# First attention: reciprocals stored element by element, output product moved, GpSimd gates removed

## The reference, cut to what matters

```python
q, k, v = einsum('bsx,xAnh->Abnsh', input, w)          # b=8, s=512, x=128, 16 heads of 64
q = q + q_bias
a = einsum('bnqh,bnkh->bnqk', q, k) * 64 ** -0.5
a = a + relative_causal(einsum('bnqh,nvh->bnqv', q, emb) * 64 ** -0.5)
a = softmax(where(lower_triangle, a, -1e9), axis=-1)
o = einsum('bnqk,bnkh->bqnh', a, v).reshape(b, s, 1024)
out = o @ (out_kernel * scale) + out_bias
x = layernorm(x + out)
```

## Time and profile before

| | |
|---|---|
| median of 3 runs | 1633.0 us (1631.59 to 1633.61) |
| the profiled execution | 1630.46 us, span 1628.7 us |
| first product of the first attention, last one | 74.78, 763.42 us |
| PE busy | 1351.0 us, 83% |
| VectorE busy | 1305.7 us, 80% |
| ScalarE busy | 947.3 us, 58% |
| GpSimd busy | 921.4 us, 57% |
| mean granted TensorE clock | 0.953 |

### The profile page before, as it was taken

The page is one execution under the profiler, slowest core; times in us unless marked ns, Lnnn a source line. Parts: engine busy times, 40 slices in busy tenths (PEclk is TensorE's granted clock), DMA queues, the critical chain, the costliest instruction groups (busy, mean ns, idle before and its releaser), DMA issues. The chain is left out here.

```text
span 1628.7 us, 36836 instructions
## 1 busy us (share of the span) xinstructions
PE 1351.0 (83%) x11495; PEld 775.6 (48%) x11495; DVE 1305.7 (80%) x2722; ACT 947.3 (58%) x1857; POOL 921.4 (57%) x1203
## 2 busy tenths in 40 slices
PE   4888888888988988886698987489899899997936
PEld 3466656655665656654366665123332333332316
DVE  3799899998999898996788888387777877777834
ACT  2676767776767767773244444157666666665631
POOL 2788988888898989896455555211221231231635
PEclk9899999999999999997699999599999999999978
DMA  5667766565666656564000000411011111101001
GB/s 153 136 152 144 146 145 145 129 154 134 147 145 144 144 139 148 131 147 100 1 1 1 0 0 0 150 48 37 29 35 34 35 32 30 40 27 32 25 8 33
DMA packets 401554, 133.51 MB, mean 82 GB/s; under 512 B 362156, under 2 KB 389793, under 8 KB 401377
## 3 DMA queue, kind: packets, MB, share of 16 engines
q1 hardware_dynamic: 398144, 128.41, 33.2%
q10 hardware_dynamic: 1824, 3.15, 0.6%
q0 software_dynamic: 1536, 1.34, 0.3%
HBM read 37.14 MB, written 13.15 MB: 31 GB/s over the span
## 5 line engine op out<-in xcount | busy, mean ns | idle before, releaser
L565 ACT ACTIVATE prob<-score_ps,nmax 128x512 f32<-128x512 f32 (+3 forms) x512 | 264.8, 525 | 202.7 <-DVE nmax L606 201.9
L1577 DVE TENSOR_REDUCE a_nm<-a_s 128x1 f16<-128x512 f32 x512 | 324.5, 687 | 52.8 <-PE a_s L1349 51.9
L1503 ACT ACTIVATE a_pt<-a_st 128x1024 f32<-128x1024 f32 x256 | 260.7, 1021 | 121.8 <-PE a_st L1367 118.7
L618 DVE SCALAR_TENSOR_TENSOR p<-prob,p 128x1280 f16<-128x1280 f32 x128 | 214.4, 1675 | 44.8 <-ACT p L574 44.8
L1349 PE MATMUL a_s<-a_kop,a_qop 128*128 128x512 f16 x512 | 198.1, 388 | 58.8 <-DVE a_nm L1577 42.3
L606 DVE TENSOR_REDUCE nmax<-score_ps 128x1 f32<-128x512 f32 (+3 forms) x512 | 217.9, 480 | 18.1 <-PE score_ps L486 15.9
L708 POOL TENSOR_TENSOR k_l<-k,k_h 64x512 f16<-64x512 f32 x130 | 191.5, 1473 | 10.9
L483 PE MATMUL score_ps<-k_h,q_h 128*128 128x512 f16 (+3 forms) x512 | 156.5, 306 | 48.5 <-ACT prob L565 28.9
L130 POOL TENSOR_TENSOR gate<-mhalf 128x1 f32<-128x1 f32 (+1 forms) x284 | 85.8, 302 | 190.5 <-ACT k L586 64.4
L708 POOL TENSOR_TENSOR q_l<-q,q_h 128x512 f16<-128x512 f32 x130 | 183.0, 1408 | 10.8
L574 ACT ACTIVATE p<-prob 128x1280 f16<-128x1280 f32 x128 | 162.6, 1271 | 8.5
(11 more groups left out here) (328 smaller groups left out, 3319.2 us busy)
## 6 DMA issues: line engine op xcount, KB each, us to landing
r_bc<-r_parts SPq DMA_DIRECT2D x128, 128.0 KB, 2.8
a_qop<-q_parts SPq DMA_DIRECT2D x32, 128.0 KB
a_kop<-k_parts SPq DMA_DIRECT2D x128, 24.0 KB
x_tok<-in_L_attn_input_dram SPq DMA_DIRECT2D x4, 512.0 KB, 12.4
pt<-p SPq DMA_TRANSPOSE x128, 4.1
r_parts<-rsum SPq DMA_DIRECT2D x128, 2.0 KB, 2.2
e_w<-in_L_ffn_w_dram SPq DMA_DIRECT2D x1, 2048.0 KB, 8.4
q_parts<-a_q_h SPq DMA_DIRECT2D x16, 128.0 KB
```

Of the source, the lines that this page charges most:

```text
L565: ins = nc.scalar.activation(prob[h][:, P_OFF[c]:P_OFF[c] + w], score_ps[u][:, col:col + w], ACT.Exp, bias=nmax[h][:, c:c + 1], accum_out= ...
L618: nc.vector.scalar_tensor_tensor(p16[h][k][:, 1, :], prob[h][:, :], P_SCALE, p16[h][k][:, 0, :], ALU.mult, ALU.subtract).then_inc(p_lo[h], 1)
L1503: nc.scalar.activation(pt[kc % 2][r][:, :, :], st_ps[r][:, :, :], ACT.Exp, scale=1.0 / SC).then_inc(exp_done[r], 1)
L1577: nc.vector.tensor_reduce(nm[g % 2][:, c, hh:hh + 1], s_ps[c % 2][:, :], AX.X, ALU.max, negate=True).then_inc(max_done[c % 2], 1)
```

## The change

Three edits. The store of the reciprocals writes DRAM in the order c, p, which makes it 512 elements of 4 bytes instead of 128 runs of 16; in return `normalise` reads `r_bc` contiguously. `normalise(n - 2)` stands ahead of `low(0, n)` on VectorE. On GpSimd the gate is gone; a semaphore increment stands in its place, and the counts that the subtractions wait for are doubled.

```diff
             def store_r(h, n, k):
...
-                sp.dma_start(r_dram[k, h].rearrange("(q c) -> q c", c=QC), rsum[h][k][:, :]).then_inc(r_stored, 16)
+                sp.dma_start(r_dram[k, h].rearrange("(c q) -> q c", q=P), rsum[h][k][:, :],
+                             allow_slow_non_contiguous=True).then_inc(r_stored, 16)
...
             def normalise(n, k):
...
-                nc.vector.tensor_tensor(o32[:, :].rearrange("p (c q) -> p c q", q=P), pv_ps[:, :].rearrange("p (c q) -> p c q", q=P),
-                                        r_bc[k][:, :].rearrange("p (q c) -> p c q", c=QC), ALU.mult).then_inc(o_done, 1)
+                nc.vector.tensor_tensor(o32[:, :], pv_ps[:, :], r_bc[k][:, :], ALU.mult).then_inc(o_done, 1)
...
                 reciprocals(0, n, k)
-                low(0, n, k)
                 if later(n, 2):
                     normalise(n - 2, k)
+                low(0, n, k)
                 maxima(1, n)
...
-            def split(rows, src, hi, lo, chain_n):
-                pool_gate(nc, m, rows)
+            def split(src, hi, lo, chain_n):
+                pool.sem_inc(pool_steps, 1)
                 nc.gpsimd.affine_select(out=hi, in_=src, compare_op=ALU.is_ge, fill=0.0, base=0,
                                         pattern=[[1, S]], channel_multiplier=0).then_inc(pool_steps, 1)
                 pool.wait_ge(pool_steps, chain_n)
...
-                split(slice(0, P), q32[h][:, :], q_h[h][:, :], q_l[h][:, :], 4 * n + 2 + 2 * h).then_inc(q_split[h], 1)
+                split(q32[h][:, :], q_h[h][:, :], q_l[h][:, :], 8 * n + 4 + 4 * h).then_inc(q_split[h], 1)
...
-                split(r, k32[r, :], m.k_h[h][r, :], m.k_l[h][r, :], 4 * n + 1 + 2 * h).then_inc(k_split[h], 1)
+                split(k32[r, :], m.k_h[h][r, :], m.k_l[h][r, :], 8 * n + 2 + 4 * h).then_inc(k_split[h], 1)
```

## The result

The changed kernel takes **2265.6 us** (median of 4 runs, 2261.8 to 2271.6); the kernel before, on the same chip, 1632.4 (4 runs, 1631.6 to 1633.6). The ratio is 1.389 [1.3875, 1.3911]: 39% slower, where 1616 us had been forecast. The profiled execution took 2271.6 us, its span 2269.9. The last product of the first attention starts at 1402.3 us instead of 763.4; that is 639 of the 641 us of loss between the two profiled executions, and the later stages keep their time.

The account below looks back on a forecast made before the run. GpSimd, with the port lock it shares with VectorE, was taken to bound steady bodies. Per batch 12.16 + 7 x 10.38 + 1.7 = 86.5 against 88.63, eight batches -16.8: 1613.7 profiled, 1616 us forecast, range 1594 to 1634.

Parts of the forecast that it names:

- The store: Reciprocals' store to DRAM, 512 elements of 4 bytes: landing 2.5 us instead of 2.2, hidden up to 5.6 us.
- rival 4: Store landing above 5.6 us makes the product wait for reciprocals: pitch 10.38 + (landing - 5.6), 1680 us at 7; chance 0.05.
- The contiguous read: VectorE's product reading reciprocals without stride: 692 ns instead of 1057, gaining 0.36 us, hidden by GpSimd in steady bodies.
- Product ahead of remainder 0: New VectorE order, product in the wait for ScalarE: yields nothing in GpSimd-bound bodies.
- Steady pitch: Distance between products in GpSimd-bound bodies of the first attention: GpSimd's own 8.20 plus 2.19 for remainders, 10.38 us.
- Gates: Four GpSimd gates a body replaced by increments: 0.10 us saved each, 0.40 a body.
- rival 3: On GpSimd's queue the increment costs what the gate did: pitch 10.79, 1639 us; chance 0.07.
- Batch end: Interval across a batch's end: product goes fully into VectorE's wait for ScalarE, 13.14 - 0.98 = 12.16 us.
- a free increment: Bound of the gate term on GpSimd: increment costs nothing, pitch 10.23, 1608 us; with statistics and norm hidden as well, 1600.
- the 1.7: Extra us per batch in bodies after its end: 1.35 for GpSimd's layer norm, 0.35 for VectorE's statistics; bounds 0 to 2.5.

Follow-up runs that it names:

- e2: The kernel before with only the store by 4-byte elements and the contiguous read, old order and gates: 2266.0 us, ratio 1.389.
- e6: The changed kernel with each stored element 64 bytes from the next, the broadcast reading an input table instead of the reciprocals: ratio 0.9937 to the kernel before.
- e4: The kernel before with only the product moved ahead of remainder 0 on VectorE: ratio 1.0016.
- e1: The changed kernel with the store and the read of before, new order and no gates kept: 1633.2 us against 1631.3 for the kernel before, ratio 1.0004.
- e8: e1 with 8 matmuls of zeros in each batch's third body and 6 in its first: 1638.96 us against 1645.59 for the kernel before, ratio 0.9961.
- e7: e1 with 8 matmuls of zeros in each batch's third body, behind the output projection: ratio 0.9977 to the kernel before.
- e5: The changed kernel with only the store undone, contiguous read kept, so reciprocals go to wrong queries: ratio 0.994 to the kernel before.
- m1: A separate program of single small transfers, each waited for, in 14 forms: 512 x 4 B in a row landed in 9.6 us, 128 x 16 B in 1.9.
- e3: The kernel before with only GpSimd's gates replaced by semaphore increments: ratio 0.9987.

## Why the prediction was wrong

**The step that failed: *The store*.** I took its landing as 2.5 us, between 2.2 (128 elements of 16 bytes, the same direction) and 4.8 (4,096 elements of 4 bytes, the other direction), "in proportion". Both rows were real; the second was of another kind of transfer. The text even said that it "writes SBUF and not DRAM, so dearer is possible", and then left the upper end at 4.8 and the chance of rival 4 at 0.05. By itself the store needs 9.6 us, the read of the same elements 2.1, and a store with 64 bytes between the elements 2.6: direction and spacing of the addresses decide, and the sum had neither. A bound from a row of the other direction is no bound, and a doubt of that kind has to go into the range.

**Rival 4 had the place, not the price.** The product does wait for r_bc. Its rule, 10.38 + (landing - 5.6), would give 14.4 with the 9.6 of a store by itself, or about 1827 us by its own sum. The missing 440 us come from the landing in the kernel, which is longer than that of a store alone: with the 14.1 us from store to broadcast the rule gives 18.9, or about 2080 us, nearer to the 20.8 measured but still short. Two stores are in flight there at a time, beside transposes that take 10.1 us to land for 4.1. How much of the 14.1 is the other store and how much are the transposes, no run separates. And the place is wider than the product: SP's loop through its own wait for the stores has the same pitch whichever instruction of VectorE is the first to wait; e2, with another order, has the same time.

The Trainium skill (DMA: Bandwidth & Descriptors, rules for kernel authors) had the direction right: keep the last dimension contiguous, or each element becomes a descriptor. The runs agree that a 4-byte element is a packet, but not that their number is the price: e6 has the same number and its stores land in 2.3 us. What costs is crowded writes.

A bound of the sum was off as well: a free increment with the 1.7 hidden gives 1608 - 13.6 = 1594, where it says 1600. Nothing hangs on it.

**What of the rest held.** *The contiguous read*: 692 ns, as said, and hidden in steady bodies, as said; its value at the batch's start (0.6%) I had put at nothing. *Product ahead of remainder 0*: nothing in steady bodies, right (10.69 and 10.84 in e4 for 10.82 before); a new wait of the product for PE's pv_ps appears (28.6 us, 39 times in 600 in e1) and costs nothing there, since GpSimd binds. Steady pitch 10.36 to 10.45, forecast 10.38: right, and with it the reading that GpSimd and the resource it shares with VectorE's remainders were the bound. *Gates*: 0.33 a body for 0.40, right in kind; rival 3, that nothing is saved, is out.

**What was mis-sized: *Batch end*.** The interval across the end is 13.10, not 12.16: the 0.98 that the product gives up is taken again by the bias and the norm, which now meet GpSimd at work. That is +0.94; what the sum had left out is that without gates GpSimd reaches them earlier, as e4 with 12.29 shows. The other seven intervals give 75.8 for 74.4, +1.4, and that is the fall of PE's clock: e8, where it doesn't come, has 10.82 for 12.26, and 74.1 for all seven. Together 88.9 for 86.5, which is why e1 gains nothing. Before, idle times of PE of 2.49 and 2.50 us passed with the clock at 1.00 in five batches of six; in the sixth, ending at 583.61, the clock was 0.50 for some 3 us and the interval 10.95 instead of 10.69. In e1 2.54 us were followed by a fall six times of seven, in e7 2.03 to 2.07 us five times of six, and in e5 2.45 us only in every second batch. The length of the idle time alone doesn't decide it, and what does is open. Open as well is why the fall lies elsewhere with the read without stride.

## What to carry to other kernels

Many small elements written side by side in DRAM were dear here, as if they went one after the other: count the writes that fall into each 64 bytes before you turn a layout on the store side, and try to rearrange on the read side instead, where 4-byte elements were cheap (2.1 against 9.6 us). A price for a transfer is only bounded by rows of the same direction and the same pattern of addresses; a slow one delayed the transposes beside it as well (10.1 for 4.1 us), so look for the loop of issues and waits that it stands in, and take its landing under load. And in a tuned loop look at what the clock of PE does behind its idle time: with the new order and no gates, a few matmuls of zeros took a batch from 88.9 to 87.2 us.

## What the runs showed of the hardware

- 512 writes of 4 bytes to DRAM land in 9.6 us when they lie in a row, in 2.6 when they lie 64 bytes apart (m1). In the kernel that is an estimated 0.31 us of packet time for each against 0.007 (after, e6). In a row with 8 bytes an element 512 of them need 4.1 us, with 16 bytes 2.7, with 64 bytes 1.8.
- The mean share of the DMA engines can pass 1 (1.33 in the changed kernel): the times of packets are added up, and they overlap. Read it together with the GB/s beside it.
- VectorE's remainder and GpSimd's operations hold each other up in e1 as in the kernel before: the subtraction at 368.20 lasts 2.42 instead of 1.16, the remainder at 416.20 1.80 instead of 1.45.
- PE's granted clock fell to 0.50 for 3 to 6 us behind idle times of 2.03 to 2.71 us (e7, e5, before, e1, e3), and at other times passed the same idle times at 1.00. A fall made its interval 1.2 to 1.7 us longer in e1, e3, e5 and e7 and 0.3 in the kernel before; in e5 the next interval gave 1.4 back.
